# Row maxima of the causal attention: turned by 32x32 blocks on VectorE and sent in twelve transfers per tile

## The chip, the cores and the metric

The kernel runs on one core of one Trainium2 chip. The metric is the device time of one execution in microseconds (us); the time of before is the median of three runs. A core has five engines with instruction streams of their own: TensorE (PE in the profile; its weight loads are shown apart as PEld), VectorE (DVE), ScalarE (ACT), GpSimd (POOL) and SyncE (SP). SyncE here only issues transfers to the 16 DMA engines. Each engine works through its own list of instructions in order, and the engines wait for each other on semaphores.

## The reference, cut to what matters

The program is a stack of two transformer layers on 2 x 2048 tokens of 256 features: causal attention with ALiBi and 16 heads, a spectral mixing layer, a channel attention, and a layer of eight experts, with a layer norm after each. The change lies in the first part:

```python
q, k, v = (proj(q_w), proj(k_w), proj(v_w))          # [b, 16 heads, 2048, 16]
scores = jnp.einsum('bhid,bhjd->bhij', q, k) / scale
alibi = -distance[None, :, :] * _slopes(N_HEADS)[:, None, None]
scores = scores + alibi[None]
scores = jnp.where(causal[None, None], scores, -jnp.inf)
attn = jax.nn.softmax(scores, axis=-1)
out = jnp.einsum('bhij,bhjd->bhid', attn, v)
```

The softmax needs the maximum of each query's row over its allowed keys. The kernel computes the scores twice: once to take the maxima, and once, transposed (keys on the partitions), to take the exponentials.

## The kernel before

**Tiles.** A unit is one batch and four heads, eight units in all. A unit has four query tiles of 512 queries, each of four blocks of 128. So there are 32 tiles, numbered t = 4 x unit + qt, from 0 to 31; with qt the number of keys grows, and a tile with qt = 3 is the largest.

**First pass (Chunk, Maxima).** For one tile PE multiplies queries by keys into a pair of PSUM banks (line 1238, with the causal mask added at 1245), and DVE reduces each pair to partial maxima (1832). When a tile's last chunk is reduced, the step Maxima makes one negated maximum per query and head (`neg_max`, 128 partitions of queries within a block, 16 columns of head and block; 1839), and POOL splits it into three bf16 parts in four short operations (2249 to 2255), so that their sum keeps the fp32 value.

**Sending (SendMaxima).** The second pass wants these maxima as three more rows of the query operand `q_op`, so that the multiplication itself subtracts the maximum. That takes a turn from partitions to columns: PE transposes the 128 x 48 parts against an identity into PSUM (1252), DVE copies the 48 x 128 result to `max_t` (1848), and SP issues three transfers, one for each part, from 16 partitions of 256 bytes into one partition row of `q_op` (2346). SendMaxima takes a pair of PSUM banks from the same ring that the chunks use.

**Second pass (Score, Weigh).** PE multiplies keys by the extended queries (1266), ACT takes the exponentials (1638), POOL masks the diagonal (2261), and PE weighs the values with them (1288). The first Score of a tile waits on PE for the semaphore of the tile's transfers:

```python
if step.first:
    pe.wait_ge(s.max_rows[t % 2], 48 * (t // 2 + 1))
```

**The order.** A planner, FrontPlan, writes one list of steps that all five engines follow. It keeps a clock for each engine and puts next what its costs say is ready. A tile's first Score may stand in the list once the planner believes the maxima are in place:

```python
LAG, PE_LAG, ROWS_LAG = 80, 190, 3000
self.sent_at[u, qt] = self.dve + self.ROWS_LAG
```

These are costs in nanoseconds that set the order and nothing else: 3000 is the time allowed from the end of DVE's copy to the landing of the three transfers. If the rows come later than the planner thought, PE stands at the Score in the list and nothing behind it runs. SP's list also holds the loads of the operands of later units (2413 to 2421), spread out by waits for Scores that have run. After the last unit's chunks the list holds the folding of the spectral weights (FoldFirst, 1205; FoldSecond), and behind the attention the back part of the program (output projection, spectral layer, channel attention, experts) follows.

Of the kernel before, what the change touches and what calls it, by code (L numbers as in the profile page):

```python
# [8 lines left out]
BF16 = mybir.dt.bfloat16  # L9
I32 = mybir.dt.int32  # L10
ALU = mybir.AluOpType
# [3 lines left out]
P = 128  # L15
# [74 lines left out]
Maxima = namedtuple("Maxima", "u qt t ring turned_before")  # L90
SendMaxima = namedtuple("SendMaxima", "u qt t ring room")
# [48 lines left out]
STRIPE = 32  # L140
UNIT_COLUMNS = GH * LENGTH * (LENGTH + P) // 2 // P


class FrontPlan:
# [6 lines left out]
    def __init__(self):  # L151
# [11 lines left out]
        self.to_send, self.to_weigh, self.to_divide, self.sums, self.middles, self.stores = [], [], [], None, [], []  # L163
        self.turned_ring, self.divided_ring, self.sums_at = {}, {}, 0
# [67 lines left out]

    def send_at(self):
        return max(self.to_send[0][-1], self.room_at()) if self.to_send else None
# [100 lines left out]
    def chunk(self):  # L335
# [122 lines left out]
    def step(self):  # L458
# [3 lines left out]
        if self.n_chunk == len(self.chunks) and not self.to_send and len(self.slots) == 2:  # L462
            self.give_room(self.slots[(self.n_room + 1) % 2])
        ready = {name: at for name, at in (("send", self.send_at()), ("divide", self.divide_at()), ("chunk", self.chunk_at()),
# [19 lines left out]
        order = ["send", "divide"]  # L484
# [15 lines left out]
        {"send": self.send, "divide": self.divide, "chunk": self.chunk, "score": self.score, "weigh": self.weigh,  # L500
# [413 lines left out]
class Memory:  # L914


    def __init__(self, nc, ctx, t, out):
# [27 lines left out]
        self.neg_max = sb("neg_max", [P, MAXIMA])  # L945
        self.max_rest = sb("max_rest", [P, MAXIMA])
        self.max_parts = [sb(f"max_parts{i}", [P, 3, MAXIMA], BF16) for i in range(2)]
        self.max_t = [sb(f"max_t{i}", [3 * MAXIMA, P], BF16) for i in range(2)]
# [124 lines left out]
class Signals:  # L1073


    def __init__(self, nc, ctx):
# [28 lines left out]
        self.negated, self.max_split = sem("negated"), sem("max_split")  # L1105
# [51 lines left out]
def tensor_front(nc, m, s, plan):  # L1157
    pe = nc.tensor
    for step in plan.steps:
# [625 lines left out]
def vector_front(nc, m, s, plan):  # L1785
# [4 lines left out]
    dve.memset(m.sums, 0.0).then_inc(s.sums_cleared, 1)  # L1790
    for step in plan.steps:
# [43 lines left out]
        elif isinstance(step, Maxima):  # L1835
            dve.wait_ge(s.ring_taken, step.ring + 1)
            if step.t:
                dve.wait_ge(s.max_split, 4 * step.t)
            dve.tensor_reduce(m.neg_max[:, :].rearrange("p (h r) -> p r h", h=GH),  # L1839
# [3 lines left out]

        elif isinstance(step, SendMaxima):
            dve.wait_ge(s.ring_filled, step.ring + 1)
# [795 lines left out]
```

## Time and profile before

| what | value |
|---|---|
| median of three runs | 1410.93 us |
| the three runs | 1408.43, 1410.93, 1414.3 us |
| span of the profiled execution, first to last instruction | 1408.5 us |
| PE busy | 1352.5 us, 96% |
| DVE busy | 1058.0 us, 75% |
| ACT busy | 868.1 us, 62% |
| POOL busy | 264.9 us, 19% |
| granted TensorE clock, mean over the span | 0.989 |

The profile gives for the profiled execution its span and no other time, so the span stands for its own time here; it lies 2.4 us under the median of the runs. Busy time of PE is a union of overlapping matmuls whose ends are modelled, so a busy PE is not one at its peak; how much work stands between two events is read better from starts. Where the timeline merges instructions, it gives the start of the first, the time to the end of the last, and their number.

### The profile page before, as it was taken

The page shows a single profiled execution, that of the slowest core. Times are in us where ns is not written, and L with a number is a line of the kernel's source. Part 1 is how long each engine was busy: PE and PEld are TensorE (multiplying, and loading weights), DVE is VectorE, ACT ScalarE, POOL GpSimd, SP SyncE. Part 2 cuts the span into 40 slices and gives each one's busy share as a digit, 9 for nine tenths or more (in the row PEclk, how much of TensorE's full clock was granted, in tenths as well). Part 3 has the DMA queues.
Part 4 walks back from the last instruction along what each step waited for, and adds up shares of the span by engine and source line. Part 5 has one row for each costly group of instructions (what it writes and reads, how often), then busy time and mean ns, then how long its engine had stood idle before and what let it go on. Part 6 is the DMA issues. An engine that isn't in the chain of part 4 may idle for free. (4 is left out here: it accounts for less than half of the span.)

```text
span 1408.5 us, 44217 instructions
## 1 busy us (share of the span) xinstructions
PE 1352.5 (96%) x18479; PEld 836.7 (59%) x18479; DVE 1058.0 (75%) x1972; ACT 868.1 (62%) x1783; POOL 264.9 (19%) x436
## 2 busy tenths in 40 slices
PE   7999999999999999999999999899987699999998
PEld 4554334444444444444454444688865589999997
DVE  2566888889888898888899880455687676766765
ACT  3445658777778777787877887654466333333332
POOL 4332011102111111021111110000257511111111
PEclk9999999999999999999999999999998899999999
DMA  7685501112211111111300000313623654445451
GB/s 225 203 208 127 95 19 35 45 34 49 46 34 47 41 42 46 34 47 41 98 9 4 4 3 2 118 36 119 228 88 137 207 201 182 175 183 183 159 186 67
DMA packets 77825, 134.10 MB, mean 95 GB/s; under 512 B 12226, under 2 KB 64443, under 8 KB 72252
## 3 DMA queue, kind: packets, MB, share of 16 engines
q1 hardware_dynamic: 59612, 108.84, 26.1%
q10 hardware_dynamic: 14608, 14.00, 3.1%
q0 software_dynamic: 3408, 8.43, 1.7%
q8 instruction: 148, 2.42, 0.7%
q14 instruction: 49, 0.40, 0.1%
HBM read 67.75 MB, written 23.11 MB: 65 GB/s over the span
## 5 line engine op out<-in xcount | busy, mean ns | idle before, releaser
L1832 DVE TENSOR_REDUCE part_max<-pair 128x2 f32<-128x1024 f32 (+2 forms) x576 | 644.6, 1162 | 63.8 <-PE pair L1238 36.1
L1638 ACT ACTIVATE big<-pair 128x512 f32<-128x512 f32 (+1 forms) x1120 | 580.5, 603 | 178.5 <-PE pair L1266 169.7
L1238 PE MATMUL pair<-big 128*32 128x512 bf16 (+3 forms) x5120 | 343.6, 349 | 5.6 <-DVE part_max L1832 5.5
L1266 PE MATMUL pair<-big 128*32 128x512 bf16 (+3 forms) x5120 | 343.8, 349 | 1.1 <-ACT big L1638 0.4
L1288 PE MATMUL pair<-big 128*17 128x512 f32 (+3 forms) x2560 | 287.4, 528 | 0.4 <-POOL big L2261 0.3
L1238 PEld LDWEIGHTS pair<-big 128*32 128x32 bf16 x5120 | 130.1, 96 | 187.8 <-DVE part_max L1832 79.3
L1266 PEld LDWEIGHTS pair<-big 128*32 128x32 bf16 x5120 | 123.6, 96 | 150.1 <-ACT big L1638 72.1
L1651 ACT ACTIVATE std<-moments,eps_col 128x1 f32<-128x1 f32 (+1 forms) x110 | 32.5, 296 | 220.6 <-DVE moments L1870 220.5
L1529 PE MATMUL pair<-big,tok 128*128 128x128 f32 x1248 | 148.6, 278 | 5.9 <-DVE big L2145 5.9
L1529 PEld LDWEIGHTS pair<-big,tok 128*128 128x128 f32 x1248 | 147.0, 194 | 10.0 <-DVE big L2145 8.3
L2261 POOL TENSOR_SCALAR_AFFINE_SELECT big<-big 128x512 f32<-128x512 f32 x128 | 80.0, 635 | 362.5 <-ACT big L1638 362.5
L1541 PE MATMUL pair<-big 128*128 x624 | 141.0, 379 | 0.0
L1541 PEld LDWEIGHTS pair<-big 128*128 128x128 f32 x624 | 115.6, 190 | 14.2
L1288 PEld LDWEIGHTS pair<-big 128*17 128x17 f32 x2560 | 68.6, 97 | 37.0 <-ACT big L1638 2.5
L1245 PE MATMUL pair<-masks,ident_b 128*32 128x64 bf16 x2048 | 85.8, 193 | 0.0
L2308 POOL DMA_INDIRECT out<-big x39 | 38.4, 984 | 251.1 <-DVE big L2186 251.1
L1245 PEld LDWEIGHTS pair<-masks,ident_b 128*32 128x32 bf16 x2048 | 53.0, 97 | 25.7 <-issue 21.0
L1350 PE MATMUL pair<-big 128*128 128x256 f32 x256 | 60.3, 389 | 3.6 <-ACT big L1667 2.6
L1181 PE MATMUL pair<-big 128*128 128x512 f32 x128 | 61.0, 624 | 0.9 <-issue 0.8
L2249 POOL CAST max_parts<-neg_max 128x16 bf16<-128x16 f32 x32 | 6.3, 196 | 292.3 <-DVE neg_max L1839 292.3
L2145 DVE TENSOR_SCALAR big<-pair,cent_columns 128x128 f32<-128x128 f32 x78 | 28.7, 407 | 38.4 <-issue 25.2
L1682 ACT ACTIVATE tok<-tok,shift,rstd 128x256 f32<-128x256 f32 x96 | 49.8, 591 | 10.7 <-DVE shift L1941 10.6
(187 smaller groups left out, 1258.4 us busy)
## 6 DMA issues: line engine op xcount, KB each, us to landing
tok<-big SPq DMA_DIRECT2D x39, 1024.0 KB, 4.7
big<-in_L_ffn_w SPq DMA_DIRECT2D x16, 1024.0 KB, 13.0
big<-split_dram SPq DMA_DIRECT2D x216, 64.0 KB, 2.8
split_dram<-big ACTq DMA_DIRECT2D x32, 384.0 KB, 3.7
big<-split_dram SPq DMA_DIRECT2D x42, 256.0 KB, 4.2
big<-routed_dram SPq DMA_DIRECT2D x39, 129.0 KB, 2.1
tok<-in_L_attn_x SPq DMA_DIRECT2D x8, 512.0 KB, 6.6
big<-in_c_query_rows SPq DMA_DIRECT2D x8, 512.0 KB, 5.1
```

Source lines behind the costliest of these rows:

```text
L1181: mm = pe.matmul(m.bank[b], m.w_qkv0[side][:, c, step.m * P:(step.m + 1) * P], m.x_t[step.tile % 2][:, c, :], start=(c == 0), stop=(c == K ...
L1238: mm = pe.matmul(bank[q:q + STRIPE, o:o + w], m.q_op[slot][:, step.qt, h, step.r * P + q:step.r * P + q + STRIPE], m.k_op[slot][:, h, step ...
L1245: mm = pe.matmul(bank[q:q + STRIPE, o + w - P + half:o + w - P // 2 + half], m.ident_b[:, q:q + STRIPE], m.masks[:, 1, half:half + P // 2] ...
L1266: mm = pe.matmul(m.bank[step.bank][k:k + STRIPE, n * w:(n + 1) * w], m.k_op[slot][:, h, step.kb * P + k:step.kb * P + k + STRIPE], m.q_op[ ...
L1288: mm = pe.matmul(m.sums[32 * h:32 * h + HD + 1, q0:TILE], m.v_aug[:, b * BPB + kb, g * GH + h, :], m.p_ring[:, place, h, at:at + TILE - q0 ...
L1350: mm = pe.matmul(m.bank[b][:, j * D:(j + 1) * D], m.turned_x[slot][:, c, r * P:(r + 1) * P], weight[:, c, :], start=(c == 0), stop=(c == K ...
L1529: mm = pe.matmul(m.bank[b][:, j * P:(j + 1) * P], w1[:, c, f * P:(f + 1) * P], m.xln_t[i % 2][:, c, :], start=(c == 0), stop=(c == KC - 1))
L1541: mm = pe.matmul(m.bank[b][:, 0:D], m.hidden_t[i % 2][:, f, :], m.w2[:, bass.ds(e, 1), f, :].rearrange("p a n -> p (a n)"), start=(f == 0) ...
L1638: act.activation(m.p_ring[:, step.place, step.heads[0]:step.heads[-1] + 1, step.at:step.at + w], m.bank[step.bank][:, 0:len(step.heads) * ...
L1682: done = act.activation(row, row, ACTF.Identity, bias=m.shift[:, j, r:r + 1], scale=m.rstd[:, j, r:r + 1])
L1832: dve.tensor_reduce(m.part_max[(step.u * QT + step.qt) % 2][:, step.r, step.heads[0]:step.heads[0] + n, step.c], banks[:, :, 0:w], X, ALU. ...
L2261: pool.affine_select(weights, weights, pattern=[[0, GH], [1, P]], compare_op=ALU.is_ge, fill=zero, base=0, channel_multiplier=-1).then_inc ...
```

## The change

The turn leaves PE. DVE transposes the 32 x 32 blocks of `neg_max` in fp32 (new operand `turned_max`, 128 x 32; of its columns 16 hold maxima and 16 are cleared once), then POOL splits the turned maxima in operations that are now 32 columns wide instead of 16. After a block transposition the queries of a block of 128 lie in four pieces of 32, one in each quarter of the partitions. So SP sends each part in four transfers, 12 per tile instead of 3, each from 16 partitions of 64 bytes. The step SendMaxima is gone: its PE transposition, its DVE copy, and its turn in the ring of PSUM pairs. SP's transfers stand at the step Maxima and wait for POOL's last split. In the planner the 200 ns of the reduction become 330 ns, and `sent_at` is POOL's end plus the same 3000 ns.

```diff
+QUADRANTS = P // STRIPE
@@ FrontPlan.chunk
-            self.steps.append(Maxima(u, qt, t, n, self.turned_ring.get(t - 2, -1) + 1))
-            self.dve += 200
+            self.steps.append(Maxima(u, qt, t, n))
+            self.dve += 330
             self.pool = max(self.pool, self.dve + self.LAG) + 1150
-            self.to_send.append((u, qt, t, self.pool + self.LAG))
-
-    def send(self):
-        u, qt, t, _ = self.to_send.pop(0)
-        n, room = self.take_ring()
-        self.turned_ring[t] = n
-        self.steps.append(SendMaxima(u, qt, t, n, room))
-        self.pe += 310
-        self.dve = max(self.dve, self.pe + self.PE_LAG) + 200
-        self.free[room.slot] = self.dve + self.LAG
-        self.sent_at[u, qt] = self.dve + self.ROWS_LAG
+            self.sent_at[u, qt] = self.pool + self.ROWS_LAG
@@ tensor_front
-        elif isinstance(step, SendMaxima):
-            pe.wait_ge(s.max_split, 4 * (step.t + 1))
-            wait_room(pe, s, step.room)
-            pe.transpose(m.bank[MAX_BANKS[step.room.slot][0]].bitcast(BF16)[0:3 * MAXIMA, 0:P],
-                         m.max_parts[step.t % 2][:, :, :].rearrange("p a n -> p (a n)"),
-                         m.ident_b[:, :]).then_inc(s.ring_filled, 1)
...
-                pe.wait_ge(s.max_rows[t % 2], 48 * (t // 2 + 1))
+                pe.wait_ge(s.max_rows[t % 2], 16 * len(MAX_ROWS) * QUADRANTS * (t // 2 + 1))
@@ vector_front
             dve.wait_ge(s.negated, step.t + 1)
-
-        elif isinstance(step, SendMaxima):
-            dve.wait_ge(s.ring_filled, step.ring + 1)
-            if step.t >= 2:
-                dve.wait_ge(s.max_rows[step.t % 2], 48 * (step.t // 2))
-            dve.tensor_copy(m.max_t[step.t % 2][:, :],
-                            m.bank[MAX_BANKS[step.room.slot][0]].bitcast(BF16)[0:3 * MAXIMA, 0:P]).then_inc(s.ring_taken, 1)
+            if step.t:
+                dve.wait_ge(s.max_split, 4 * step.t)
+            dve.transpose(m.turned_max[:, :], m.neg_max[:, :]).then_inc(s.max_turned, 1)
@@ pool_front
-            pool.tensor_copy(parts[:, 0, :], m.neg_max[:, :]).then_inc(s.max_split, 1)
+            pool.tensor_copy(parts[:, 0, :], m.turned_max[:, :]).then_inc(s.max_split, 1)
@@ sync_front
-        elif isinstance(step, SendMaxima):
-            sp.wait_ge(s.ring_taken, step.ring + 1)
+        elif isinstance(step, Maxima):
+            sp.wait_ge(s.max_split, 4 * (step.t + 1))
             for a, row in enumerate(MAX_ROWS):
-                sp.dma_start(m.q_op[step.u % 3][row:row + 1, step.qt, :, :].rearrange("o h n -> o (h n)"),
-                             m.max_t[step.t % 2][a * MAXIMA:(a + 1) * MAXIMA, :]).then_inc(s.max_rows[step.t % 2], 16)
+                to = m.q_op[step.u % 3][row:row + 1, step.qt, :, :].rearrange("o h (r n) -> o (h r) n", r=BPT)
+                for k in range(QUADRANTS):
+                    sp.dma_start(to[:, :, k * STRIPE:(k + 1) * STRIPE],
+                                 m.max_parts[step.t % 2][k * STRIPE:k * STRIPE + MAXIMA, a, :]
+                                 ).then_inc(s.max_rows[step.t % 2], 16)
```

Since the planner's clocks run on without SendMaxima, the whole list of the front is written anew. Three places follow, each with the rows of before and then those of the changed kernel. Line numbers in the changed kernel differ: 1226 and 1233 are the chunks, 1247 is Score, 1269 Weigh.

On SP, around tiles 7 and 8 of the front, `max_t` marks the three transfers of a tile, and lines 2419 and 2421 are loads of later operands. Before:

```order
L2421 DMA big<-split_dram 16x4x512 x4
L2419 DMA big<-split_dram 16x4x2048
L2346 DMA big<-max_t 1x16x128 x3
L2421 DMA big<-split_dram 16x4x512 x3
L2346 DMA big<-max_t 1x16x128 x3
L2421 DMA big<-split_dram 16x4x512
```

The same place on SP in the changed kernel:

```order
L2401 DMA big<-split_dram 16x4x2048
L2403 DMA big<-split_dram 16x4x512 x4
L2327 DMA big<-max_parts 1x16x32 x12
L2401 DMA big<-split_dram 16x4x2048
L2403 DMA big<-split_dram 16x4x512 x2
L2327 DMA big<-max_parts 1x16x32 x12
L2403 DMA big<-split_dram 16x4x512 x2
```

Each tile's three transfers have become twelve, from another tile of SBUF, and the loads that stood between tiles 7 and 8 stand there still.

On DVE, at the maxima of tile 7, before:

```order
L1839 TENSOR_REDUCE neg_max<-part_max 128x4x4
L1832 TENSOR_REDUCE part_max<-pair 128x4 x2
L1832 TENSOR_REDUCE part_max<-pair 128x2
L1848 COPY max_t<-pair 48x128
L1832 TENSOR_REDUCE part_max<-pair 128x2 x3
```

The same place on DVE in the changed kernel:

```order
L1822 TENSOR_REDUCE neg_max<-part_max 128x4x4
L1828 STREAM_TRANSPOSE turned_max<-neg_max 128x32
L1815 TENSOR_REDUCE part_max<-pair 128x4 x2
L1815 TENSOR_REDUCE part_max<-pair 128x2 x4
```

The copy behind three chunk reductions is gone, and a transposition stands directly behind the reduction of the maxima.

On PE, at the first Score of tile 31, the last tile (`pair` is a PSUM bank; line 1205 is FoldFirst), before:

```order
L1288 MATMUL pair<-big 17x512 x4
L1266 MATMUL pair<-big 32x384 x8
L1252 MATMUL pair<-ident_b,max_parts 48x128
L1288 MATMUL pair<-big 17x512 x4
L1266 MATMUL pair<-big 32x384 x4
L1266 MATMUL pair<-big 32x256 x16
L1266 MATMUL pair<-big 32x128 x16
L1288 MATMUL pair<-big 17x512 x4
L1288 MATMUL pair<-big 17x384 x4
L1205 MATMUL pair<-big 128x256 x16
L1266 MATMUL pair<-big 32x512 x16
```

The same place on PE in the changed kernel, from the end of the last chunk (1233) on; the first Score of tile 31 is the 32x512 row behind the 32x128 row:

```order
L1233 MATMUL pair<-masks,ident_b 32x64 x4
L1269 MATMUL pair<-big 17x512 x8
L1247 MATMUL pair<-big 32x512 x24
L1269 MATMUL pair<-big 17x512 x4
L1247 MATMUL pair<-big 32x384 x12
L1269 MATMUL pair<-big 17x512 x4
L1247 MATMUL pair<-big 32x384 x4
L1247 MATMUL pair<-big 32x256 x16
L1269 MATMUL pair<-big 17x512 x4
L1247 MATMUL pair<-big 32x128 x16
L1247 MATMUL pair<-big 32x512 x12
```

The transposition (line 1252) is gone, and the sixteen matmuls of FoldFirst no longer stand ahead of tile 31's first Score; they come later.

## Rows read from the trace of the kernel before

**Rows 1.** The page, part 2: busy tenths of PE, and PE's granted clock in tenths.

```profile
PE   7999999999999999999999999899987699999998
PEclk9999999999999999999999999999998899999999
```

**Rows 2.** Busy time by stretch: us, PE, PEld, DVE, ACT, POOL, clock, DMA share, GB/s.

```profile
200.00:300.00 100.00, 99.99 (x2000) 45.32 (x1996) 89.77 (x91) 79.75 (x155) 13.27 (x32) 1.00 0.16 37
```

**Rows 3.** Waits: engine and line, what ended them, total us, times, longest.

```profile
PEld pair L1266 <- DMA big<-max_t: 2.6, 7, 0.5
```

**Rows 4.** Timeline of tile 7: start, duration, engine, line, operation, count, idle before.

```profile
277.41 0.22 DVE L1839 TENSOR_REDUCE neg_max<-part_max 128x16 f32<-128x64 f32 x1
278.53 0.22 POOL L2255 TENSOR_TENSOR max_parts<-max_rest,max_parts 128x16 bf16<-128x16 f32 x1
280.09 0.24 PE L1252 MATMUL pair<-ident_b,max_parts 128*48 128x128 bf16 x1
280.26 0.51 PE L1266 MATMUL pair<-big 128*32 128x384 bf16 x8
280.61 1.79 SPq L2346 DMA_DIRECT2D big<-max_t  x3
284.95 0.61 PE L1266 MATMUL pair<-big 128*32 128x512 bf16 x8
```

**Rows 5.** Timeline of tile 11, whose first Score starts at 378.28.

```profile
370.54 0.22 DVE L1839 TENSOR_REDUCE neg_max<-part_max 128x16 f32<-128x64 f32 x1
373.75 2.80 SPq L2346 DMA_DIRECT2D big<-max_t  x3
377.42 1.03 PE L1288 MATMUL pair<-big 128*17 128x512 f32 x8
378.28 0.39 PE L1266 MATMUL pair<-big 128*32 128x512 bf16 x4
378.50 0.60 PE L1238 MATMUL pair<-big 128*32 128x512 bf16 x8
378.93 0.39 PE L1266 MATMUL pair<-big 128*32 128x512 bf16 x4
```

**Rows 6.** Transfers of the maxima: count, issue ns min/median/max; landing from issue.

```profile
L2346 SPq DMA_DIRECT2D big<-max_t x96: 523/590/1954, 62.2 to 845.9; - x96
DMA to landing us min/median/max: 1.7/2.2/3.8
```

**Rows 7.** SP's issues of the first unit's operand loads: ns min/median/max.

```profile
L2392 SPq DMA_DIRECT2D big<-split_dram x24: 316/426/1229, 21.6 to 70.1; - x24
```

**Rows 8.** POOL's subtraction on 512 columns: ns min/median/max.

```profile
L2241 POOL TENSOR_TENSOR big<-big x32: 1153/1157/1166, 15.1 to 131.0; 128x512 bf16<-128x512 f32 x32
```

**Rows 9.** Timeline: final reductions and first Scores of tiles 0, 2, 3 and 31.

```profile
58.18 0.18 DVE L1839 TENSOR_REDUCE neg_max<-part_max 128x16 f32<-128x16 f32 x1
...
68.19 0.39 PE L1266 MATMUL pair<-big 128*32 128x512 bf16 x4
...
144.87 0.20 DVE L1839 TENSOR_REDUCE neg_max<-part_max 128x16 f32<-128x48 f32 x1
...
152.34 0.83 PE L1266 MATMUL pair<-big 128*32 128x512 bf16 x12
...
183.81 0.22 DVE L1839 TENSOR_REDUCE neg_max<-part_max 128x16 f32<-128x64 f32 x1
...
190.40 1.07 PE L1266 MATMUL pair<-big 128*32 128x512 bf16 x8
...
842.54 0.22 DVE L1839 TENSOR_REDUCE neg_max<-part_max 128x16 f32<-128x64 f32 x1
...
854.78 1.05 PE L1266 MATMUL pair<-big 128*32 128x512 bf16 x16
```

**Rows 10.** Busy time by stretch around a fall of the granted clock.

```profile
185.30:188.70 3.40, 1.61 (x50) 0.78 (x46) 2.84 (x5) 0.00 (x0) 0.00 (x0) 1.00 0.01 1
188.80:192.20 3.40, 3.17 (x44) 1.02 (x34) 3.26 (x4) 1.10 (x3) 0.83 (x4) 0.50 0.01 2
```

More of the change, by code:

```diff
@@ L89 @@
 Chunk = namedtuple("Chunk", "u qt r heads c width per_bank ring room")
-Maxima = namedtuple("Maxima", "u qt t ring turned_before")
-SendMaxima = namedtuple("SendMaxima", "u qt t ring room")
+Maxima = namedtuple("Maxima", "u qt t ring")
 Score = namedtuple("Score", "u qt kb q0 heads n bank before ring_clear first place at")
@@ L231, in weigh_at @@
         return at
-    def send_at(self):
-        return max(self.to_send[0][-1], self.room_at()) if self.to_send else None
     def divide_at(self):
@@ L461, in step @@
             self.give_room(2)
-        if self.n_chunk == len(self.chunks) and not self.to_send and len(self.slots) == 2:
+        if self.n_chunk == len(self.chunks) and len(self.slots) == 2:
             self.give_room(self.slots[(self.n_room + 1) % 2])
-        ready = {name: at for name, at in (("send", self.send_at()), ("divide", self.divide_at()), ("chunk", self.chunk_at()),
+        ready = {name: at for name, at in (("divide", self.divide_at()), ("chunk", self.chunk_at()),
                                            ("score", self.score_at()), ("weigh", self.weigh_at()),
@@ L483, in step @@
         two = len(self.to_weigh) > 1 and self.to_weigh[1][-1] <= self.pe
-        order = ["send", "divide"]
+        order = ["divide"]
         ahead = 700 if self.max_columns - self.score_columns > 0.5 * UNIT_COLUMNS else 1200
@@ L499, in step @@
         self.pe = max(self.pe, first)
-        {"send": self.send, "divide": self.divide, "chunk": self.chunk, "score": self.score, "weigh": self.weigh,
+        {"divide": self.divide, "chunk": self.chunk, "score": self.score, "weigh": self.weigh,
          "project": self.project, "fold": self.fold}[name]()
@@ L944, in __init__ @@
         self.part_max = [sb(f"part_max{i}", [P, BPT, GH, 4]) for i in range(2)]
[L945 to L948, printed above, removed]
+        self.neg_max = sb("neg_max", [P, STRIPE])
+        self.turned_max = sb("turned_max", [P, STRIPE])
+        self.max_rest = sb("max_rest", [P, STRIPE])
+        self.max_parts = [sb(f"max_parts{i}", [P, 3, STRIPE], BF16) for i in range(2)]
         self.recip_l = sb("recip_l", [P, 2 * BPT, GH])
@@ L1104, in __init__ @@
         self.ring_filled, self.ring_taken = sem("ring_filled"), sem("ring_taken")
-        self.negated, self.max_split = sem("negated"), sem("max_split")
+        self.negated, self.max_turned, self.max_split = sem("negated"), sem("max_turned"), sem("max_split")
+        self.max_cleared = sem("max_cleared")
         self.scored, self.exped, self.weighed = sem("scored"), sem("exped"), sem("weighed")
@@ L1790, in vector_front @@
     dve.memset(m.sums, 0.0).then_inc(s.sums_cleared, 1)
+    dve.memset(m.neg_max[:, :], 0.0).then_inc(s.max_cleared, 1)
+    dve.wait_ge(s.max_cleared, 1)
     for step in plan.steps:
@@ L1837, in vector_front @@
             if step.t:
-                dve.wait_ge(s.max_split, 4 * step.t)
-            dve.tensor_reduce(m.neg_max[:, :].rearrange("p (h r) -> p r h", h=GH),
+                dve.wait_ge(s.max_turned, step.t)
+            dve.tensor_reduce(m.neg_max[:, 0:MAXIMA].rearrange("p (h r) -> p r h", h=GH),
                               m.part_max[step.t % 2][:, :, :, 0:step.qt + 1], X, ALU.max,
@@ L2245, in pool_front @@
             t, parts = step.t, m.max_parts[step.t % 2]
-            pool.wait_ge(s.negated, t + 1)
+            pool.wait_ge(s.max_turned, t + 1)
             if t >= 2:
-                pool.wait_ge(s.ring_filled, step.turned_before)
-            pool.tensor_copy(parts[:, 0, :], m.neg_max[:, :]).then_inc(s.max_split, 1)
+                pool.wait_ge(s.max_rows[t % 2], 16 * len(MAX_ROWS) * QUADRANTS * (t // 2))
+            pool.tensor_copy(parts[:, 0, :], m.turned_max[:, :]).then_inc(s.max_split, 1)
             pool.wait_ge(s.max_split, 4 * t + 1)
-            pool.tensor_tensor(m.max_rest[:, :], m.neg_max[:, :], parts[:, 0, :], ALU.subtract).then_inc(s.max_split, 1)
+            pool.tensor_tensor(m.max_rest[:, :], m.turned_max[:, :], parts[:, 0, :], ALU.subtract).then_inc(s.max_split, 1)
             pool.wait_ge(s.max_split, 4 * t + 2)
```

4 lines of the change are left out of this document (2 added, 2 removed).

## The prediction

> **What bounds the kernel now.** I read the page first. From the second slice to the 25th, some 35 to 880 us, PE is busy nine tenths or more in every slice, and the clock is full in tenths [rows 1], and in the stretch from 200 to 300 us it is busy 99.99 of 100 us, with DVE at 90 and ACT at 80 [rows 2]; the five stretches up to 800 us look alike. So in this part of the program a microsecond of PE work taken away is worth about a microsecond, and one in which PE stands still costs one. The waits say how near PE is to standing still for the maxima: the first Score of a tile waited for the landing of their transfers 7 times, 2.6 us in all, 0.5 at the longest [rows 3]. Small as it is, this row decides the case. The planner puts that Score as early as its costs allow, so the way from the last reduction to the landed rows has next to no slack in some tiles, and what makes it longer comes out as idle PE.
>
> The timeline of tile 7 shows the way [rows 4]: the reduction starts at 277.41, POOL ends its splits at 278.75 (1.34 us on), PE transposes at 280.09, DVE copies, SP starts to issue at 280.61, and the first Score starts at 284.95, 7.54 us after the reduction. The wait row says what kept it: the landing. In tile 11 it is 7.74 us, from 370.54 to 378.28, with the same kind of work between [rows 5].
>
> **The new way, step by step.** I count from the start of the last reduction.
> - Reduction and POOL's four splits: 1.34 us, as now [rows 4].
> - DVE's transposition of 128 x 32. No such row exists. The reduction to `neg_max` next to it takes 0.22 us, and with the handover I add 0.3. It takes the place of a copy of the same length, so DVE's sum doesn't move.
> - POOL's operations on 32 columns in place of 16. The subtraction takes 1.16 us on 512 columns [rows 8] and 0.22 on 16 [rows 4], so 1.9 ns a column and 0.03 for 16 more, 0.12 for four. Were each to double, it would be 0.8.
> - PE's transposition, DVE's copy and the waits between, from 278.75 to 280.61 in tile 7, fall away: 1.86 us saved.
> - SP's issues. Three transfers take 1.79 us [rows 4], the first 0.52 and each further one 0.63 with its gap. Issued on one queue they are serial, so the last of twelve starts 0.52 + 0.04 + 10 x 0.63 = 6.9 us after the first (the last of three: 1.2). Some issues are held up: the median is 0.59 us but the longest 1.95 [rows 6], and tile 11's three took 2.80 [rows 5]. With such a stop in about every third tile of three transfers, twelve catch one or two; I add 0.7.
> - Landing: median 2.2 us after its issue began, 1.7 to 3.8 [rows 6]. The 64-byte pieces move less than the 256-byte ones, 16 pieces per transfer either way, so I leave it.
>
> Sum: 1.34 + 0.3 + 0.12 + 0.06 + 6.9 + 0.7 + 2.2 = 11.6 us, against 7.5 with three transfers. The bounds are 10.4 (no stop, landing 1.7) and 14 (POOL doubled, stops of 1.5, landing 3). Nine more issues outweigh what leaving PE saves. The planner doesn't know it: its 3000 ns from POOL's end stand for 9.8 us.
>
> **What PE does meanwhile**, tile by tile. Unit prices from starts in tile 11 [rows 5]: a Weigh of 512 columns 0.86 us, a Score of one head and 512 columns 0.22, a chunk of two heads 0.43.
> - Tiles 11, 15, 19, 23, 27: the order keeps the work between last chunk and first Score as it was, but for the transposition. Work covers 7.74 - 0.3 = 7.4 us, so PE idles 4.2 in each. Tiles like 7 and 15 waited up to 0.5 already, so I count 20 us for the five, not 21.
> - Tile 7: one chunk, four Scores and one Weigh fewer stand between (0.43 + 0.88 + 0.86 = 2.2 us). 7.54 - 0.5 - 0.3 - 2.2 = 4.5 us of cover, 7.1 idle, less the 0.5 of now: 6.6 us.
> - Tile 31: now 12.24 us pass [rows 9], FoldFirst among them, and nothing waits for the maxima. In the new order FoldFirst comes behind. Left are 5 Weighs and 13 Scores, 4.3 + 2.6 = 6.9 us after the last chunk, of which 1.9 pass before the reduction starts. Idle: 11.6 - 5.0 = 6.6 us.
> - The first unit. Tile 0 has 10.0 us now [rows 9]; in the new order one Project and two chunks fewer stand between, and cover shrinks to 3.7 us: 7.9 idle, less 1.3 idle now, 6.6. Tile 1 (98.39 to 107.92 by the same view, rows not shown) loses about 2 of its 9.5 us of cover while operand loads share the queue, for which I make its way 12.5: 4.9. Tile 2: the way grows by 4.1 beyond the 7.47 of now [rows 9], with 0.4 more work: 3.7. Tile 3 takes 6.59 us now [rows 9]: 5.0 longer, and 1.0 of work moved away: 6.0. Together 21.2 us.
> - The other 20 tiles have 10 us or more between landing and use and don't wait. Their twelve transfers push the next operand loads back by up to 5.7 us; those loads are spread over a unit and end tens of microseconds ahead of their first use, which hides it.
>
> Idle PE in all: 20 + 6.6 + 6.6 + 21.2 = 54.4 us.
>
> **What the change gives.** On PE the transposition starts at 280.09 and the next matmul at 280.26 [rows 4]: 0.17 us, and I allow 0.08 around it for the turn out of fp32 matmuls. 32 x 0.25 = 8 us. Below is 5.4 (0.17 alone); above, if every idle stretch of the weight loads ahead of it counted, some 26, for which nothing in the matmuls' starts speaks. The ring place set free lets a chunk go in sooner, but there the limit is PE's own work; I take nothing.
>
> **The clock.** Where PE was busy 1.61 of 3.40 us, around tile 3, the clock granted in the next 3.4 us was 0.50, 1.2 GHz in place of 2.4 [rows 10]. The eleven gaps of 4 to 8 us are emptier than that one was. A stretch of 3.4 us at half costs at most 1.7 us of work, less where it lies partly in the gap. I take 0.65 on average, 7 us (0 to 19).
>
> **Sum:** 54.4 - 8 + 7 = 53.4 us. On the profiled span of 1408.5 that is 1461.9; the median lies 2.4 above it, so I say **1464 us**. The part behind 880 us doesn't change.
>
> **A rule against the rows.** What an issue costs is the largest term. The rows say 0.59 us for these transfers; loads from DRAM issued one behind another take a median of 0.43 [rows 7]. The Trainium skill, DMA: Bandwidth & Descriptors, section "Queues, rings and completion order", gives 512 sequencer cycles per plain copy for generations before the newest, and Advanced Engine Details and Errata, "Clock Domains", 1.2 GHz for SP's sequencer, thus an estimate of 0.43 us; by it the sum would come to about 1440. The trace agrees for the loads, not for the transfers of the maxima.
>
> **Rivals.**
> 1. *Cheap issues.* Twelve of them might cost 0.43 with a gap of 0.04, as the loads do [rows 7]. The way is 10 x 0.16 plus a little, 2 us, shorter; eleven tiles give 22 us back and the clock 2 more: 1440 us. Against it: the 96 transfers of now have a median of 0.59 and a minimum of 0.52 [rows 6]. Chance 0.14.
> 2. *Dear issues or landings.* Pieces of 64 bytes into a strided row, twelve at a time, may meet the stop of tile 11 each time: at 0.95 us an issue the way is 3.2 longer, 35 us over eleven tiles: about 1500. For it: stops exist with only three in a row. Chance 0.16.
> 3. *The planner's allowance holds* (the other side). If the twelve land within 7.4 us of the reduction, tiles 11 to 27 don't wait, and with some slack elsewhere only the 8 us of PE work remain: 1402 us. This decides from an issue price of 0.3 us, or if PE ran so late against the list that the maxima had time. The seven waits of now say that it doesn't run late [rows 3], and no issue of these was under 0.52. Chance 0.04; and 0.03 that waits and savings cancel near 1411.
> 4. My forecast, 1445 to 1490: 0.63.
>
> The range, 1430 to 1502, takes in rivals 1 and 2 nearly whole. A measurement of this kernel tells about 0.5%, 7 us. Faster than that: 0.04; within: 0.03; slower: 0.93.
>
> **What would show it.** In the trace after, the first Scores of tiles 7, 11, 15, 19, 23, 27 and 31 and of the first unit should wait for `max_parts` transfers, 4 us or more each, 45 to 60 in all; twelve issues should take 7.5 us or more; the stretches of 100 us should show PE at 95 or 96 in place of 100, with the clock under 1.00; and the part behind the attention should keep its length. If the issues take 5.5, rival 1 is right. I am wrong if the wait row stays at a few microseconds: then the issues are cheap or the Score isn't just in time.

## The result: 4% slower, about as forecast

| | before | after |
|---|---|---|
| median | 1410.14 us (1408.43 to 1414.3, 4 runs) | 1465.87 us (1464.89 to 1467.26, 4 runs) |
| ratio, 95% interval | | 1.0393 (1.0377 to 1.0409) |
| span of the profiled execution | 1408.5 us | 1464.3 us |
| granted clock, mean | 0.989 | 0.971 |

The forecast was 1464 us. It came out within 2 us, but not because every term was right: three of them were off, one effect was not in the sum at all, and the errors cancelled, as the experiments show.

**The page of after** (busy time by engine, and PE and its clock in 40 slices), which answers to [rows 1]:

```profile
span 1464.3 us, 44383 instructions
PE 1363.2 (93%) x18447; PEld 844.7 (58%) x18447; DVE 1059.1 (72%) x1973; ACT 861.6 (59%) x1783; POOL 267.0 (18%) x436
PE   7898779989999999999899998999997699999998
PEclk9999999999999999999999999999999799999999
```

DVE's sum has hardly moved, so its transposition costs what the copy cost. PE shows eights and sevens between the second and the 25th slice where it had none before.

**PE's longest waits** (what PE waited for: us in total, times, longest), and the wait of the weight loads (PEld) for the same transfers, which answers to [rows 3]:

```profile
PE pair L1247 <- DMA big<-max_parts: 50.5, 11, 6.5
PE pair L1358 <- ACT masks L1654: 7.0, 6, 3.2
PE pair L1158 <- DMA tok<-in_L_attn_x: 6.6, 1, 6.6
```

```profile
PEld pair L1247 <- DMA big<-max_parts: 57.4, 11, 7.0
```

PE now stands 50.5 us, eleven times, at a tile's first Score, and what ends the wait each time is the landing of the maxima. All other waits of PE are as small as before. The eleven tiles are those of the forecast: 0 to 3, 7, 11, 15, 19, 23, 27 and 31. In the kernel before, PE's matmuls never stood for the maxima: the 2.6 us of [rows 3] are waits of the weight loads alone, and they passed under matmuls that still ran.

**The timeline of tile 11** (start, duration, engine, line, instruction; in brackets the idle time before it and what ended it), which answers to [rows 5]:

```profile
400.99 0.22 DVE L1822 TENSOR_REDUCE neg_max<-part_max 128x16 f32<-128x64 f32 x1
401.25 0.21 DVE L1828 STREAM_TRANSPOSE turned_max<-neg_max 128x32 f32<-128x32 f32 x1
...
401.52 0.21 POOL L2228 CAST max_parts<-turned_max 128x32 bf16<-128x32 f32 x1 [21.58 <-DVE turned_max L1828]
...
402.42 0.25 POOL L2234 TENSOR_TENSOR max_parts<-max_rest,max_parts 128x32 bf16<-128x32 f32 x1
...
402.69 8.34 SPq L2327 DMA_DIRECT2D big<-max_parts  x12
...
407.54 1.03 PE L1269 MATMUL pair<-big 128*17 128x512 f32 x8
...
412.18 0.40 PE L1247 MATMUL pair<-big 128*32 128x512 bf16 x4 [3.61 <-DMA big<-max_parts]
```

The way, from the start of the last reduction to the start of the first Score, has three parts. To the first issue it is now 1.70 us; then SP issues for 8.34 us; 1.15 us after the last issue's end PE starts the Score. PE's last Weigh had ended by 408.57, and after it PE had nothing that the list allows it to do. Issuing takes three quarters of the 11.19 us.

**Issues and POOL's splits** (minimum, median, maximum in ns), which answer to [rows 6]:

```profile
L2327 SPq DMA_DIRECT2D big<-max_parts x384: 523/589/1748, 59.5 to 900.6; - x192
L2228 POOL CAST max_parts<-turned_max x32: 208/209/211, 58.3 to 892.1; 128x32 bf16<-128x32 f32 x32
```

The price of one issue, 0.59 us, is that of before; there are four times as many. POOL's CAST takes 0.21 us on 32 columns.

**Stretches of after** (busy us of PE, PEld, DVE, ACT and POOL with instructions, then the granted clock, DMA's share and GB/s), the first of which answers to [rows 2]:

```profile
200.00:300.00 100.00, 91.47 (x1760) 40.65 (x1763) 83.18 (x85) 68.79 (x132) 11.10 (x28) 0.97 0.16 30
700.00:800.00 100.00, 95.26 (x1896) 44.93 (x1888) 84.59 (x85) 73.64 (x146) 13.46 (x32) 0.98 0.20 45
408.60:412.10 3.50, 0.00 (x0) 0.00 (x0) 0.88 (x1) 0.00 (x0) 1.92 (x6) 1.00 0.02 2
413.10:416.40 3.30, 3.30 (x56) 1.41 (x52) 1.89 (x2) 1.71 (x4) 0.00 (x0) 0.50 0.66 86
947.00:1464.30 517.30, 481.81 (x3103) 426.72 (x3103) 352.75 (x1242) 226.20 (x550) 114.34 (x139) 0.97 0.44 155
```

PE does nothing from 408.6 to 412.1, and the clock granted in that stretch is still 1.00. Then it works through the whole of the following stretch at a granted clock of 0.50, 1.2 GHz in place of 2.4. The part behind the attention takes 517.3 us, and took 518.0 before (890.5 to 1408.5), so all of the 56 us were lost in the attention part.

### The profile page after: what moved, and what is told of

The parts are those of the page before. It is cut to its first block and busy times, and to the rows that moved or that the text cites. A ratio compares the mean times of both kernels' runs of the same rounds, so it can differ in the third digit from the quotient of the medians.

```text
span 1464.3 us, 44383 instructions
## 1 busy us (share of the span) xinstructions
PE 1363.2 (93%) x18447; PEld 844.7 (58%) x18447; DVE 1059.1 (72%) x1973; ACT 861.6 (59%) x1783; POOL 267.0 (18%) x436
## 5 line engine op out<-in xcount | busy, mean ns | idle before, releaser
L1247 PE MATMUL pair<-big 128*32 128x512 bf16 (+3 forms) x5120 | 346.2, 355 | 50.7 <-DMA big<-max_parts 50.5
L1226 PE MATMUL pair<-big 128*32 128x512 bf16 (+3 forms) x5120 | 349.0, 352 | 4.5 <-DVE part_max L1815 4.3
L1269 PE MATMUL pair<-big 128*17 128x512 f32 (+3 forms) x2560 | 294.2, 539 | 0.9 <-POOL big L2240 0.6
L1247 PEld LDWEIGHTS pair<-big 128*32 128x32 bf16 x5120 | 126.9, 97 | 209.9 <-ACT big L1619 72.9
L1226 PEld LDWEIGHTS pair<-big 128*32 128x32 bf16 x5120 | 134.3, 98 | 193.9 <-DVE part_max L1815 70.6
L1233 PEld LDWEIGHTS pair<-masks,ident_b 128*32 128x32 bf16 x2048 | 54.2, 99 | 31.1 <-issue 24.3
L2228 POOL CAST max_parts<-turned_max 128x32 bf16<-128x32 f32 x32 | 6.7, 209 | 334.2 <-DVE turned_max L1828 334.2
L2124 DVE TENSOR_SCALAR big<-pair,cent_columns 128x128 f32<-128x128 f32 x78 | 28.4, 406 | 38.2 <-issue 27.2
```

Source lines behind the costliest of these rows:

```text
L1226: mm = pe.matmul(bank[q:q + STRIPE, o:o + w], m.q_op[slot][:, step.qt, h, step.r * P + q:step.r * P + q + STRIPE], m.k_op[slot][:, h, step ...
L1233: mm = pe.matmul(bank[q:q + STRIPE, o + w - P + half:o + w - P // 2 + half], m.ident_b[:, q:q + STRIPE], m.masks[:, 1, half:half + P // 2] ...
L1247: mm = pe.matmul(m.bank[step.bank][k:k + STRIPE, n * w:(n + 1) * w], m.k_op[slot][:, h, step.kb * P + k:step.kb * P + k + STRIPE], m.q_op[ ...
L1269: mm = pe.matmul(m.sums[32 * h:32 * h + HD + 1, q0:TILE], m.v_aug[:, b * BPB + kb, g * GH + h, :], m.p_ring[:, place, h, at:at + TILE - q0 ...
```

## The experiments

Ratios are to the kernel before on the same chip; the three groups of runs were made on different chips, one of which ran the kernel before in 1418.7 us, so only ratios are compared between groups.

### 1. The changed kernel with a planner that knows the way

The only edit is the planner's allowance, in the changed kernel:

```diff
-    LAG, PE_LAG, ROWS_LAG = 80, 190, 3000
+    LAG, PE_LAG, ROWS_LAG = 80, 190, 9500
```

> The changed kernel with one number altered: the planner's allowance for the rows to land is 9500 ns in place of 3000. It sets only the order. Theory (the twelve serial issues are late against an order that believes in 3 us): the work between last chunk and first Score grows from 9.0 to 12.8 us in tiles 7, 11, 15, 19, 23, 27, FoldFirst comes back ahead of tile 31, and the waits for the transfers fall from 50.5 us to about 10, left in tiles 2 and 3, where there is not enough work to put between. Time 1405 to 1420 us, so within 0.7% of before. Rival (the changed kernel is slower because of what the transfers or the transposition do to the other engines): the time stays above 1445 us although the waits go.

Measured: 1410.6 us (10 runs), ratio 1.0007 (0.9987 to 1.0028). The twelve transfers are as slow as they were. In tile 11 (splits, issues):

```profile
370.05 0.21 POOL L2228 CAST max_parts<-turned_max 128x32 bf16<-128x32 f32 x1 [20.66 <-DVE turned_max L1828]
...
370.95 0.24 POOL L2234 TENSOR_TENSOR max_parts<-max_rest,max_parts 128x32 bf16<-128x32 f32 x1
371.22 8.05 SPq L2327 DMA_DIRECT2D big<-max_parts  x12
```

And PE's wait for them is nearly gone (us in total, times, longest). The expectation had 10 us left in tiles 2 and 3; what is left stands in tiles 23 and 27:

```profile
PE pair L1247 <- DMA big<-max_parts: 2.0, 2, 1.4
```

So the whole loss is a matter of order. Nine more issues per tile cost nothing when 9.5 us of other work stand ahead of the Score, and 4% when 3 us were allowed for. It also bounds what the change gives. With the waits gone, the stretch from the reduction of tile 8 to that of tile 16 takes 187.6 us against 188.4 before, about 0.1 us for each of the eight transpositions that PE is spared. From tile 7 to tile 27 it is 470.1 against 469.9, and 2.0 us of waits of PE stand in the 470.1, so 0.1 us each again, as far as two single profiles can tell. The run as a whole is no faster than the kernel before.

### 2. Twelve transfers alone, with PE's transposition kept

In the kernel before, each row of the maxima is sent in four pieces (the waits count 192 in place of 48):

```diff
             for a, row in enumerate(MAX_ROWS):
-                sp.dma_start(m.q_op[step.u % 3][row:row + 1, step.qt, :, :].rearrange("o h n -> o (h n)"),
-                             m.max_t[step.t % 2][a * MAXIMA:(a + 1) * MAXIMA, :]).then_inc(s.max_rows[step.t % 2], 16)
+                to = m.q_op[step.u % 3][row:row + 1, step.qt, :, :].rearrange("o h (r n) -> o (h r) n", r=BPT)
+                for k in range(4):
+                    sp.dma_start(to[:, :, k * 32:(k + 1) * 32],
+                                 m.max_t[step.t % 2][a * MAXIMA:(a + 1) * MAXIMA, k * 32:(k + 1) * 32]
+                                 ).then_inc(s.max_rows[step.t % 2], 16)
```

> The kernel before, with PE's transposition and DVE's copy kept, but each of the three rows of maxima sent in four transfers of 16 x 64 bytes, twelve per tile. Theory (issue count on one queue): the way grows by 9 x 0.63 = 5.7 us, waits of PE for the transfers 50 us in all (5.2 to 5.7 in tiles 7 to 27, some 19 in the first unit, none in tile 31), and with the clock's falls 1460 to 1475 us. Rival (what costs is the new route through DVE and POOL or the planner's new order): at most 1425 us.

Measured: 1481.24 us (1479.47 to 1482.21), ratio 1.0502 (1.0484 to 1.052). It is slower than the changed kernel, and above the range that was expected. The number of transfers alone makes more than the whole loss, so neither DVE's transposition nor POOL's wider splits are its cause. Its waits (us in total, times, longest) and its tile 11:

```profile
PE pair L1266 <- DMA big<-max_t: 50.0, 10, 5.5
```

```profile
404.34 0.22 DVE L1839 TENSOR_REDUCE neg_max<-part_max 128x16 f32<-128x64 f32 x1
...
405.48 0.22 POOL L2255 TENSOR_TENSOR max_parts<-max_rest,max_parts 128x16 bf16<-128x16 f32 x1
...
407.04 0.24 PE L1252 MATMUL pair<-ident_b,max_parts 128*48 128x128 bf16 x1
...
407.31 0.22 DVE L1848 COPY max_t<-pair 48x128 bf16<-48x128 bf16 x1
...
407.55 8.97 SPq L2348 DMA_DIRECT2D big<-max_t  x12
...
417.68 0.62 PE L1266 MATMUL pair<-big 128*32 128x512 bf16 x4 [5.42 <-DMA big<-max_t]
```

The first issue starts 3.21 us after the reduction, 1.70 in the changed kernel. POOL ends at 405.70, but PE's transposition has its place in PE's list and starts at 407.04. So the turn on VectorE makes the way 1.5 us shorter. It comes out as shorter waits in tiles 11, 15, 19, 23 and 27, which wait 25.7 us here and 18.2 in the changed kernel. In tiles 0 to 3 and 7, where the two lists hold other work, the waits are 24.3 us here and 27.2 there, and tile 31 waits in the changed kernel alone, 5.2 us. In all, PE waits as long in both, 50.0 and 50.5 us. Of the 15 us between the two kernels, the clock, at half for 68 us in place of 51, makes some 5 (at the price of run 5), and the 32 transpositions 2 to 3. The rest, some 8 us, isn't in the waits; run 6 comes back to it.

### 3. Two queues for the twelve

In the changed kernel SP issues six of the transfers, and ACT the other six, at a place among its exponentials:

```diff
+        if isinstance(step, Maxima):
+            due.append([step, 3])
+        elif isinstance(step, Score):
+            if due:
+                due[0][1] -= 1
+            while due and (due[0][1] <= 0 or (step.first and due[0][0].t <= step.u * QT + step.qt)):
+                sent = due.pop(0)[0]
+                act.wait_ge(s.max_split, 4 * (sent.t + 1))
+                send_rows(act, m, s, sent, (2, 3))
...
+            send_rows(sp, m, s, step, (0, 1))
```

> The changed kernel with half of the twelve transfers issued by ScalarE (its own queue, three Scores after the maxima or at the tile's first Score) and half by SP. Theory (serial issue): the last of six starts 3.8 us sooner on SP, so the waits fall from 50.5 us to 10 to 20 and the time to 1415 to 1430 us, unless ACT's six issues of 0.6 us each, 115 us over the front, make ACT late: then ACT's queue shows up in the waits of PE. Rival (landing of many small pieces is slow, whoever issues them): waits stay above 40 us and the time above 1450 us.

Measured: 1617.37 us (1615.17 to 1620.46), ratio 1.1469 (1.1447 to 1.149). The expectation was off by 190 us. The issuing did become shorter, as this piece of its timeline shows:

```profile
453.65 3.70 SPq L1589 DMA_DIRECT2D big<-max_parts  x6
453.66 4.00 ACTq L1589 DMA_DIRECT2D big<-max_parts  x6
...
457.71 2.56 ACT L1638 ACTIVATE big<-pair 128x512 f32<-128x512 f32 x5 [5.67 <-issue]
...
458.36 1.11 PE L1247 MATMUL pair<-big 128*32 128x512 bf16 x8 [4.86 <-ACT big L1638]
```

Six issues on each queue take 4 us in place of 8. But ACT stands for them: its exponential starts 5.67 us late (4.0 us of issues, and before them 1.6 us for POOL's last split, which they too must wait for), the banks stay full, and PE waits 4.86 us for ACT. That happens in nearly every tile, also in the 21 that waited for nothing in the changed kernel (us in total, times, longest):

```profile
ACT big L1638 <- issue: 162.0, 29, 6.7
PE pair L1247 <- ACT big L1638: 134.0, 28, 5.7
```

PE's wait for the transfers themselves fell to 14.7 us in 3 tiles, so the serial issue was cut as meant. It gave back 36 us of waits and cost 134 us of others, and the mean granted clock fell from 0.971 to 0.938. The Trainium skill (DMA: Bandwidth & Descriptors, "Issuing engines are not separate DMA queues") says of what several issuing engines save that it is "usually small relative to the DMA itself". These rows differ from it: for 1 KB transfers the issuing is 8 us of an 11 us way, and six issues hold an engine for 4 us.

### 4. PE kept busy while it waits

In the changed kernel twelve matmuls without effect (identity by identity, 512 columns, into the bank that the Score then fills) stand ahead of the wait in the eleven waiting tiles:

```diff
+            if step.first:
+                if t < 4 or t % 4 == 3:
+                    for _ in range(12):
+                        pe.matmul(m.bank[step.bank], m.ident_b[:, :], wide(m.ident_b[:, :], [P, 4, P], 1),
+                                  start=True, stop=True)
+                pe.wait_ge(s.max_rows[t % 2], 16 * len(MAX_ROWS) * QUADRANTS * (t // 2 + 1))
```

> The changed kernel with twelve idle matmuls of 512 columns (2.6 us at full clock, results overwritten) on PE ahead of the wait in tiles 0 to 3, 7, 11, 15, 19, 23, 27 and 31. They are shorter than the shortest wait, 3.2 us, so they should end before the rows land and cost nothing by themselves. If the falls of the granted clock after each wait are a cost of their own, they go, the front's clock stays 1.00, and the time falls by 7 to 16 us to 1450 to 1459; this measures the term I put at 7 us. If the clock's falls cost nothing because the work behind a wait isn't bound by PE, the time stays within 3 us of 1466.

Measured: 1453.06 us (1452.11 to 1453.74), ratio 1.0301 (1.0284 to 1.0318), 0.9% or 13 us less than the changed kernel's ratio. More work on PE makes the kernel faster, since the time is idle anyway and only the clock behind it is changed. The mean clock rose from 0.971 to 0.987.

### 5. The same, fitted to each tile's gap

```diff
-                    for _ in range(12):
+                    for _ in range({0: 24, 1: 13, 2: 26, 3: 22, 7: 21, 23: 17, 31: 20}.get(t, 12)):
```

> The changed kernel with idle matmuls ahead of each wait as before, but their number fitted to each tile's wait (24 in tile 0, 13, 26, 22 in tiles 1 to 3, 21 in tile 7, 17 in tile 23, 20 in tile 31, 12 in the others). With twelve everywhere 13.6 us at half clock were left in the front, of 51.2, and the time fell by 12.8 us. If the clock's falls cost 0.34 us per microsecond at half, the rest gives 3 to 5 us more: a ratio to before of 1.026 to 1.028, and no fall of the clock in the front. If the rest gives nothing, the ratio stays at 1.030.

Measured: 1449.77 us (1446.73 to 1450.76), ratio 1.0279 (1.0263 to 1.0294). Stretches of the attention part, of the changed kernel:

```profile
60.00:212.00 152.00, 125.82 (x1641) 60.43 (x1640) 98.42 (x107) 68.89 (x127) 31.60 (x46) 0.94 0.48 111
212.00:380.00 168.00, 161.75 (x3148) 73.49 (x3152) 141.46 (x141) 125.77 (x244) 22.84 (x52) 0.96 0.20 36
380.00:560.00 180.00, 173.03 (x3440) 80.90 (x3434) 155.38 (x157) 134.29 (x264) 24.42 (x60) 0.99 0.21 39
560.00:740.00 180.00, 172.07 (x3401) 80.32 (x3395) 152.99 (x152) 133.01 (x261) 21.11 (x52) 0.98 0.24 44
740.00:960.00 220.00, 207.10 (x3511) 101.45 (x3504) 142.29 (x162) 157.56 (x314) 28.30 (x62) 0.98 0.09 27
```

and two of them with the fitted matmuls:

```profile
60.00:212.00 152.00, 141.88 (x1770) 67.39 (x1773) 99.72 (x109) 71.33 (x132) 31.60 (x46) 1.00 0.52 113
212.00:380.00 168.00, 167.16 (x3281) 76.75 (x3281) 147.41 (x146) 130.01 (x253) 22.83 (x52) 1.00 0.20 36
```

In the changed kernel a mean of 0.94 over 152 us is 18 us at half clock; over the five stretches it makes about 51 us. With the fitted matmuls the clock is 1.00 in all five. The difference of the ratios, 1.0393 - 1.0279 = 0.0114, is 16 us: that is the clock's part of the loss, 1.5 us for each gap and 0.31 us for each microsecond at half. The other 2.8% is what the waiting costs, less what the change gives.

### 6. Twelve transfers alone, PE kept busy

Run 2 with 18 such matmuls in its ten waiting tiles (tiles 0 to 3, 7, 11, 15, 19, 23, 27), to see whether the clock was why it lost more than the changed kernel.

> The kernel before with twelve transfers of 16 x 64 bytes and eighteen idle matmuls (3.9 us) ahead of the wait in the ten tiles that wait. With the transfers alone it was 71 us slower (ratio 1.050) with 50.0 us of waits and 75 us at half clock in the front, while the changed kernel was 56 us slower with 50.5 us of waits and 51 us at half clock. If the clock makes that difference, the ratio falls to 1.033 to 1.039 here, near that of the changed kernel with its clock kept up (1.030 less what is left there), and the difference between the two shrinks from 15 us to under 8. If it is something in PE's transposition and the ring, the difference stays near 15 us.

Measured: 1462.39 us (1462.01 to 1463.1), ratio 1.0373 (1.0357 to 1.0389). It gained 0.0129, about 18 us, but stays 0.0094, 13 us, above run 5. So the clock is not what sets the two apart. Nor are the gaps. The waits that are left are, in run 5 and here (us in total, times, longest):

```profile
PE pair L1251 <- DMA big<-max_parts: 10.5, 11, 1.7
```

```profile
PE pair L1270 <- DMA big<-max_t: 10.6, 10, 1.9
```

The matmuls without effect start 0.216 us apart. The 191 of run 5 fill 41.3 us, the 180 of this run 38.9. With the waits that makes gaps of 51.8 us in run 5 and 49.5 here. But the span of run 5 is only 38.8 us longer than before (1447.3 against 1408.5), that of this run 51.9 (1460.4). The kernel with PE's transposition pays its gaps in full; the changed kernel gets 13 us of them back. The transpositions account for 2 to 3 of these. Some 4 are waits of PE for other engines, mostly for DVE's reductions, between the reductions of tiles 0 and 7 (4.3 us in run 5, 7.8 before, 8.1 here). The other 6 to 7 stay open.

### 7. Two pieces in place of four

Run 2 with two transfers of 16 x 128 bytes for each row, so six per tile (`for k in range(2)`, 64 columns each).

> The kernel before, with each row of maxima sent in two transfers of 16 x 128 bytes, six per tile. Theory (each further issue delays the first Score by 0.63 us where it is just in time): the way is 1.9 us longer than with three, PE's waits for the transfers 12 to 17 us in ten tiles, some 3 us of clock, 1422 to 1432 us. Rival (a threshold, such as the twelve transfers filling a queue, or 64-byte pieces): 1415 us or less.

Measured: 1437.84 us (1435.85 to 1438.29), ratio 1.0132 (1.0108 to 1.0156). By the ratio it is 19 us slower, and 12 to 22 were expected. PE's wait for the transfers is 14.4 us in the same ten tiles, 2.8 at the longest. So the loss grows with the number of issues: three none, six 1.3%, twelve 5%. From six to twelve the wait grows by 35.6 us over ten tiles, 3.6 us each, near the six issues of 0.63 us.

### 8. Twelve transfers of larger pieces

As run 2, but cut by heads: each transfer has 4 pieces of 256 bytes in place of 16 of 64.

```diff
+                for h in range(GH):
+                    sp.dma_start(m.q_op[step.u % 3][row:row + 1, step.qt, h, :],
+                                 m.max_t[step.t % 2][a * MAXIMA + h * BPT:a * MAXIMA + (h + 1) * BPT, :]
+                                 ).then_inc(s.max_rows[step.t % 2], 16)
```

> The kernel before with twelve transfers per tile again, but cut by heads: each takes 4 partitions of 256 bytes in place of 16 of 64. Theory (the count of issues costs, not the pieces): issues of 0.52 to 0.59 us, waits near 50 us, 1470 to 1490 us, as with twelve transfers of 16 x 64 bytes (1481). Rival (small pieces are what is slow): issue and landing shorter, waits under 35 us, under 1455 us.

Measured: 1479.72 us (1478.06 to 1480.53), ratio 1.0425 (1.0399 to 1.0451). Its issues (minimum, median, maximum in ns), and those of run 2:

```profile
L2347 SPq DMA_DIRECT2D big<-max_t x384: 593/594/1177, 61.6 to 912.7; - x192
```

```profile
L2348 SPq DMA_DIRECT2D big<-max_t x384: 523/590/1852, 61.5 to 922.7; - x192
```

An issue costs the same 0.59 us with a quarter of the pieces. Only the long stops are shorter (1.18 us at most, 1.85 with 64-byte pieces), and PE's waits are 43.5 us in place of 50.0. So 0.8% of run 2's 5% hangs on how a transfer is cut into pieces, and the rest on there being twelve.

### 9. PE's transposition five times

In the kernel before, each transposition is done five times over, 128 more in all.

> The kernel before with PE's transposition of the maxima run five times in a row in each tile (same operands, same result), 128 transpositions more. If one costs what I took for it, 0.25 us, the time grows by 32 us to 1442; if only its array time of some 0.06 us counts, by 7 us to 1417; that tells what leaving 32 of them out can give at most.

Measured: 1425.11 us (1424.47 to 1426.95), ratio 1.0044 (1.0028 to 1.0061): 6.2 us for 128, 0.05 us each. Back to back they may be cheaper than alone; run 1 has 0.1. Thirty-two of them are worth 1.6 to 3 us, not 8.

### 10. Issue each part as soon as it is split

The changed kernel with an allowance of 8600, and SP waiting for the split of each of the three parts on its own:

```diff
-            sp.wait_ge(s.max_split, 4 * (step.t + 1))
             for a, row in enumerate(MAX_ROWS):
+                sp.wait_ge(s.max_split, 4 * step.t + (1, 3, 4)[a])
```

> The changed kernel with the planner's allowance at 8600 ns, and SP issuing each part's four transfers as soon as POOL has that part, so the first issue starts 0.9 us sooner. Theory: the way from the last reduction to the landing shrinks by 0.9 us to 10.1, the order covers it in all tiles but those of the first unit, and PE's waits for the transfers stay under 5 us: 1404 to 1412 us, the same as before or a little faster, since the transpositions saved on PE are worth 0.1 us each at best.

Measured: 1415.15 us (12 runs), ratio 0.9967 (0.9954 to 0.998), with 5.7 us of waits left in six tiles, where under 5 were expected.

### 11. The same with the allowance of run 1

The change of run 10 with 9500 in place of 8600.

> The changed kernel with each part's transfers issued as soon as POOL has that part, and the planner's allowance at 9500 ns in place of 8600. The waits of PE for the transfers, 5.7 us at 8600, fall under 1 us. The time is that of before or up to 0.6% faster (ratio 0.993 to 0.999): the five microseconds of waits less, unless the order itself, with scores later, costs as much.

Measured: 1406.64 us (1403.57 to 1408.98, 11 runs), ratio 0.9977 (0.9968 to 0.9986). In tile 11 SP starts before POOL has ended:

```profile
370.70 8.38 SPq L2327 DMA_DIRECT2D big<-max_parts  x12
371.36 0.25 POOL L2234 TENSOR_TENSOR max_parts<-max_rest,max_parts 128x32 bf16<-128x32 f32 x1
```

and PE waits for the maxima once, 0.7 us. Runs 10 and 11 are the only versions faster than the kernel before, by 0.2 to 0.3%. Their intervals overlap, so which of the two is the better isn't settled. The 3 to 5 us are near what 32 transpositions on PE are worth, but it isn't shown that they are those: run 1 has the whole change and measures no gain. The kernel before with a larger allowance was not run either, so how much is due to the new order is open.

## Why the prediction was right, and where its terms were not

**What bounds the kernel.** Right. PE is the bound in the attention, its first Score stands just in time, and the planner's 3000 ns decide. Run 1 shows it: one number in the planner takes back all of the 56 us. One row was misread: [rows 3] is a row of the weight loads, not of PE's matmuls, which didn't stand at all.

**The way.** Forecast 11.6 us; measured over the eleven tiles 10.4 to 12.3, mean 11.0. By parts: to the first issue 1.82 forecast, 1.70 measured. The twelve issues with their gaps and stops 8.1 forecast (6.9 to the start of the last, 0.7 for stops, and its own 0.5), 7.5 to 9.4 measured. So the 0.7 for stops was a good guess (mean 8.1). The landing is the part that was off: 2.2 forecast from [rows 6], but PE started its Score 1.15 us after the last issue's end, about 1.7 after its start.

**Idle PE by tile.** The tiles were right, all eleven and no other. The sizes, in us:

| tiles | forecast | measured |
|---|---|---|
| 11, 15, 19, 23, 27 | 20 | 3.61, 3.36, 3.20, 4.74, 3.26: 18.2 |
| 7 | 6.6 | 5.3 |
| 31 | 6.6 | 5.2 |
| 0 to 3 | 21.2 | 6.08, 3.59, 6.48, 5.74: 21.9 |
| all | 54.4 | 50.5 |

Since no matmul of PE waited for the maxima before, nothing is to be taken off, and the term was 3.9 us too large. The way, 0.6 us shorter in eleven tiles, explains that and more. Tile 1 was put too high by 1.3 and tile 2 too low by 2.8. For tile 31 the prediction counts 13 Scores; the list in "The change" has 18 of one head, most of them narrower than 512 columns, and by columns they do come to the 2.6 us of the sum. The tiles that don't wait are 21, not 20. PE's busy time of "95 or 96" of 100 us came out from 700 to 800, but from 200 to 300, with tile 3's gap of 5.74 us, it is 91.5.

**What the change gives.** This term was wrong: 8 us forecast, 1.6 to 3 measured (runs 9 and 1). The step that failed is "0.17 us, and I allow 0.08 around it". It took the distance of two matmul starts in [rows 4] as the price of the transposition and rounded up. Run 9's 0.05 and run 1's 0.1 us lie below even the 0.17 behind the lower bound of 5.4 us.

**The clock.** Also wrong: 7 us forecast, 16 measured (runs 4 and 5), within the bounds of 0 to 19. The mechanism was right, and so was the level of 0.50. What failed is "I take 0.65 on average" per gap, which took the one stretch of 3.4 us in [rows 10] for the length of every slow stretch and halved the loss again. The 51 us at half after eleven gaps are 4.7 us per gap, and each gap lost 1.5 us.

**The sum.** The gain was 5 to 6 us too large and the clock 9 too small, which put the forecast some 14 too low; the idle term put it 3.9 too high. The measured terms make 50.5 + 16 less 2 to 3, some 64 us, where the spans are 55.8 apart. So about 8 us, 0.7 for each gap, are given back, and the prediction has no term for it. Gaps in PE's work don't give it by themselves, since in run 6, with gaps as long, nothing comes back. About 3 of the 8 are PE's other waits between the reductions of tiles 0 and 7 (4.6 us in the changed kernel, 7.8 before). For the rest no run isolates a cause, and it stays open. The forecast of 1464 was a right mechanism with sizes that happened to cancel: that it came within 2 us is luck.

**The rule against the rows.** The Trainium skill (DMA: Bandwidth & Descriptors), with its 512 cycles, gave an estimate of 0.43 us an issue, and about 1440 us by it. The figure stands there in the section "Why a DMA increments its semaphore by 16 and not by 1", not in the one that the prediction names. In 384 issues the trace shows a median of 0.59, and the measured time is 1466, so the row was the better price; run 8 shows that the number of pieces isn't what makes the difference.

**The rivals.** Cheap issues: no, median 0.59. Dear issues: stops exist (1.75 us at most), but twelve issues took 9.4 us at the longest, not 11; the rival's 35 us didn't come. The allowance holds: no, eleven waits. It would have held with 9500 in place of 3000.

**The part behind the attention** kept its length, 517.3 against 518.0 us, as forecast.

## What to carry to other kernels

Before work is moved from an engine to more transfers, count the issues: on one queue they are serial, and their number lengthens the way to the last landing, far more than how they are cut (runs 7 and 8). If a planner or a hand-written order holds an allowance for that way, change the allowance with the way; the same instructions were 3.9% slower or no slower by that number alone. A small instruction taken from the bounding engine can be worth far less than it looks in the timeline (here 0.05 to 0.1 us in place of 0.25), so measure it by doing it several times over before building on it. And when a forecast comes true, check its terms one by one: here three were off and a fourth was missing, and the sum hid it.

## What the runs showed of the hardware

- A 1 KB transfer inside SBUF costs its queue 0.59 us to issue, with 16 pieces of 64 bytes as with 4 of 256 (384 issues each), and 0.63 from start to start. The two queues of SP and ACT issue side by side, six each in 3.7 and 4.0 us, but ACT computes nothing while it issues.
- After eleven gaps of 3.2 to 6.5 us in PE's work the granted clock stood at 0.50 for 4.7 us each on average, at a loss of 1.5 us each. With matmuls without effect in the gaps it stayed at 1.00, and the kernel was 16 us faster (run 5).
- VectorE's 32x32 transposition of 128 x 32 fp32 took 0.21 us, as long as the reduction of 16 columns beside it.
- A 128 x 48 transposition on PE cost 0.05 us when repeated, though the next matmul starts 0.17 us behind it.
